# The drive factors of a selective scan: from two VectorE products to one GpSimd product per group

## The reference, cut to what matters

```python
x = _silu(conv(x_in @ W_in[:, :256]))        # u, 256 channels
delta = softplus(x @ W_dt + b_dt)
dA  = exp(delta_t[:, :, None] * A[None])     # 16 states of each channel
dBu = delta_t[:, :, None] * B_t[:, None, :] * u_t[:, :, None]
h = dA * h + dBu                             # step after step over 256 tokens
y = einsum('bds,bs->bd', h, C_t)
out = ((y + x * D) * _silu(z)) @ W_out + inp
```

## Time and profile before

| | |
|---|---|
| time before | 1379.05 us, median of 3 runs (1378.56 to 1383.14) |
| the profiled execution | 1382.59 us, span 1380.8 us |
| mean granted TensorE clock in it | 0.834 of full |
| scan phase | up to about 522 us of the span |
| a group of the scan phase | 59.8 us (from the gating at 99.82 to that at 458.65, six groups) |
| DVE busy over the span | 983.4 us (71%) |
| POOL busy over the span | 807.8 us (59%) |

### The profile page before, as it was taken

How to read it: one execution, slowest core, us unless ns; L and a number is a source line. 1 busy time by engine, 2 the same in 40 slices (tenths; PEclk the granted TensorE clock), 3 DMA queues, 4 the chain that set the end, 5 groups by cost and what they waited for, 6 DMA issues and landing times. The chain is left out here.

```text
span 1380.8 us, 15697 instructions
## 1 busy us (share of the span) xinstructions
PE 1053.1 (76%) x4347; PEld 505.1 (37%) x4347; DVE 983.4 (71%) x1673; ACT 704.0 (51%) x1392; POOL 807.8 (59%) x784
## 2 busy tenths in 40 slices
PE   6879788897988665675754778877877788649996
PEld 2334233342423223353531334333433333325554
DVE  3899999999999996656431545565666665338997
ACT  3657475675857533233331344454445453448773
POOL 1999898989989963353424333444444431237773
PEclk9899899999989896677865677787888787769998
DMA  5553241533325104000001221121122111000001
GB/s 194 220 192 155 91 185 63 214 129 148 155 91 196 51 0 90 1 0 0 0 0 46 80 60 47 58 77 52 46 60 78 47 47 47 2 0 1 16 16 31
DMA packets 34545, 103.05 MB, mean 75 GB/s; under 512 B 3611, under 2 KB 22171, under 8 KB 23707
## 3 DMA queue, kind: packets, MB, share of 16 engines
q1 hardware_dynamic: 34484, 102.35, 21.4%
HBM read 93.03 MB, written 8.91 MB: 74 GB/s over the span
## 5 line engine op out<-in xcount | busy, mean ns | idle before, releaser
L545 PE MATMUL m_yac<-m_hC,ident 128*128 128x512 f32 x512 | 283.9, 674 | 76.6 <-DVE m_hC L311 58.7
L510 POOL TENSOR_TENSOR m_dBu<-m_du,m_Bt 128x512 f32<-128x512 f32 x256 | 318.2, 1271 | 9.5 <-DVE m_du L316 8.8
L1275 ACT ACTIVATE a_pT<-a_s 128x512 f32<-128x512 f32 x256 | 150.6, 598 | 221.9 <-PE a_s L1326 221.7
L1098 DVE TENSOR_REDUCE a_nm<-a_s 128x2 f32<-128x512 f32 x256 | 163.1, 683 | 139.7 <-PE a_s L1326 136.2
L302 DVE TENSOR_TENSOR_SCAN m_dA<-m_dA,m_dBu 128x512 f32<-128x512 f32 x184 | 220.0, 1215 | 15.9 <-ACT m_dA L448 14.7
L545 PEld LDWEIGHTS m_yac<-m_hC,ident 128*128 128x128 f32 x512 | 95.2, 207 | 244.7 <-DVE m_hC L311 134.6
L448 ACT ACTIVATE m_dA<-m_delta,mprm 128x510 f32<-128x510 f32 x256 | 169.0, 673 | 0.2
L1326 PE MATMUL a_s<-qs,ks 99*128 99x256 bf16 x512 | 108.7, 307 | 44.4 <-DMA qs<-a_nmT 37.6
L1326 PE MATMUL a_s<-ks,qs 72*128 72x256 bf16 x512 | 113.5, 331 | 29.5 <-DVE a_nm L1098 18.5
L311 DVE TENSOR_TENSOR m_hC<-m_dA,m_Ct 128x512 f32<-128x512 f32 x184 | 122.6, 666 | 0.0
L445 ACT ACTIVATE m_dA<-m_zero 128x2 f32<-128x2 f32 x181 | 31.1, 172 | 166.9 <-DVE m_hC L311 166.9
(11 more groups left out here) (211 smaller groups left out, 1897.1 us busy)
## 6 DMA issues: line engine op xcount, KB each, us to landing
m_Bt<-bcd SPq DMA_DIRECT2D x32, 1024.0 KB, 5.6
m_Ct<-bcd SPq DMA_DIRECT2D x32, 1024.0 KB, 6.6
qs<-parts SPq DMA_DIRECT2D x16, 576.0 KB
ks<-parts SPq DMA_DIRECT2D x48, 192.0 KB
parts<-a_part SPq DMA_DIRECT2D x32, 192.0 KB, 2.3
out<-x_all SPq DMA_DIRECT2D x8, 256.0 KB, 2.3
mprm<-in_mprm SPq DMA_DIRECT2D x1, 1203.0 KB, 6.5
vx<-in_vrow SPq DMA_DIRECT2D x3, 256.0 KB
```

Source lines behind the costliest of these rows:

```text
L510: nc.gpsimd.tensor_tensor(dBu[:, g % RD], du[:, n % 2, c], Bt[:, s], ALU.mult).then_inc(drive_ready, 1)
L545: return nc.tensor.matmul(out, lhsT, rhs, start=start, stop=stop)
L1098: nc.vector.tensor_reduce(nm[:, q, 2 * pair:2 * pair + 2], s1[i % 2][:], AX.X, ALU.max, negate=True).then_inc(max_ready, 1)
L1275: nc.scalar.activation(pT[:, u // 2, u % 2], s2[u % 2][:], ACT.Exp, scale=float(HD) ** -0.25).then_inc(exp_ready, 1)
```

## The change

The sum of delta becomes one instruction on POOL for both halves of the channels. The drive factor moves from DVE to POOL, one instruction for both halves as well, two units behind the sum (at i = 28; in the first group directly behind the sum). The semaphores are raised by 2 at once, so that their counts are the same.

```diff
 # DVE queue
-            def drive_factor(m, c):
-                dve.wait_ge(delta_ready, CH * m + c + 1)
-                nc.vector.tensor_tensor(du[:, m % 2, c], delta[:, m % 2, c], u[:, m % 2, c],
-                                        ALU.mult).then_inc(du_ready, 1)
...
-            for c in range(CH):
-                drive_factor(0, c)
...
-                    if i in (27, 28) and n + 1 < GROUPS:
-                        drive_factor(n + 1, i - 27)
 # POOL queue
-            def sum_delta(m, c):
+            def sum_delta(m):
                 pool.wait_ge(sp_step, 7 * m + 7)
-                nc.gpsimd.tensor_tensor(delta[:, m % 2, c], sp_a[:, c], sp_r[:, c], ALU.add).then_inc(delta_ready, 1)
+                nc.gpsimd.tensor_tensor(delta[:, m % 2], sp_a[:], sp_r[:], ALU.add).then_inc(delta_ready, CH)
+
+            def drive_factor(m):
+                pool.wait_ge(delta_ready, CH * (m + 1))
+                nc.gpsimd.tensor_tensor(du[:, m % 2], delta[:, m % 2], u[:, m % 2], ALU.mult).then_inc(du_ready, CH)
...
-            for c in range(CH):
-                sum_delta(0, c)
+            sum_delta(0)
+            drive_factor(0)
...
-                    if i in (26, 27) and n + 1 < GROUPS:
-                        sum_delta(n + 1, i - 26)
+                    if i == 26 and n + 1 < GROUPS:
+                        sum_delta(n + 1)
+                    if i == 28 and n + 1 < GROUPS:
+                        drive_factor(n + 1)
```

## The result

The kernel after takes 1383.53 us (median of 12 runs) where the kernel before takes 1379.04 us in runs beside it: ratio 1.0032, 95% interval 1.0019 to 1.0044. The change costs 4.5 us; 6.3 us were forecast. The span of the profiled execution is 1381.8 us.

The account below looks back on a forecast made before the run. The group period was taken as bound by POOL's gapless queue from product 13, then factors, drives, shift, scan 31, PE's accumulation and gating. 6 x 0.88 + 1.0 = 6.3 us on 1379.05 gave 1385.4 us; range 1371.5 to 1390.

Parts of the forecast that it names:

- The price of the wide instructions: On POOL, one 1024-element instruction was taken at 2.32 us, from a line between 512 and 1120 elements.
- POOL's queue sets the period: At the six group changes behind groups 1 to 6, POOL's longer queue makes each period 0.88 us longer, 5.3 us together.
- The shift takes the place of the factors: Before scan 31, DVE's shift is held until POOL idles after drive 3, lasting some 4.7 us in place of 0.44.
- Rival (a): At the group changes, shift enters at the next end of a POOL instruction; faster, 1372 us, chance 0.23.
- Group 0: First group, without a shift: POOL is the bound and the gating behind it comes later, taken as +1.0 us.
- PE's clock: PE's accumulation before the gating: waits of about 1.04 us in three of six groups may move, -3.1 to +3.1, taken as 0.
- rival (b): Before the gating, PE waits vanish in all groups while six changes cost 0.88 us each; no change, 1382.3 us, chance 0.12.
- The sum: Whole kernel: 6 x 0.88 + 1.0 = 6.3 us slower, forecast 1385.4 us, chance 0.58.
- it runs in POOL's first idle moment: A DVE instruction with two SBUF inputs doesn't run while POOL passes between instructions without idling; shift would last some 4.7 us.

## Why the prediction was right, and where it was not

- *The price of the wide instructions* (2.36 us, from a line between two sizes): measured 2.35 and 2.36. Their gain over two narrow ones, 0.11 to 0.14 us, is in line with the run with the wide sum alone.
- *POOL's queue sets the period, up by 0.88 us:* from product 13 to product 31 it was 0.85 us. With half a factor more, 1.15 of 1.19 us appeared in this stretch.
- *The shift takes the place of the factors as the instruction that is held, 4.7 us:* 4.79 to 4.82 us. This was the step on which the sign hung, and the pause and the one-tensor form showed it by taking it away: 14 and 16 us less than the kernel after. Rival (a) had 1372 us for exactly this case; both forms came out 3 to 5 us below.
- *Group 0, +1.0 us:* the gating starts at 100.48 in place of 99.82, +0.7, inside the 100.0 to 101.0 of the forecast.
- *PE's clock, taken as 0, bounds of 3.1 us to either side:* behind groups 1 to 6 it was -0.6 us. This also decides against rival (b), whose 1382.3 us is nearer to the measured 1383.5 us than the forecast's 1385.4: it needs all of these waits gone, and 2.57 of 3.14 us are still there. The same term came out at +2.1 us in the run with the halves (5.25 against 3.14 us). Where in the group PE's clock changes level is the one part of this kernel's time that I can't work out from a diff.
- *The sum:* the last gating of the six groups starts 463.69 - 458.65 = 5.0 us later in the trace, and the runs differ by 4.5 us, with an interval of 2.6 to 6.1 us; 6.3 lies just above it. The terms as measured, 6 x 0.85 + 0.7 - 0.6 = 5.2 us, give the trace; that the runs show somewhat less is not explained by them.

The way it was reasoned was right in what it needed and wrong in its wording: "it runs in POOL's first idle moment". Four of the runs show the shift entering between two back-to-back instructions of POOL: those with the pause for the factors, the shift behind scan 31, the earlier pause, and half a factor more. And the number of tensor inputs does not draw the line: the statistics' instruction, with one, was held for 6.73 us once. The Trainium skill, "SBUF — State Buffer", section "Who interferes with whom", says that issue order decides who blocks. The traces agree in so far as POOL's instruction had started first wherever a DVE instruction was held. If POOL has instructions issued ahead of the one that runs, an exclusive port served in order of issue would pass over DVE as long as those last, and a stop would clear them; that would agree with the runs with a recent stop. It is a guess: no run here shows what POOL has issued ahead, and two places don't fit easily, the sixth change of the run with half a factor more and the statistics that were held in one group and not in the next at the same distances. What decides whether a boundary opens behind a long run of POOL stays open.

## What to carry to other kernels

Before work is moved from DVE to POOL, look for small DVE instructions that read two SBUF tensors: a POOL queue that has lost its last pause can hold one of four elements for several microseconds, and the profile books that as busy time of DVE. Compare the duration of such an instruction with that of its like elsewhere, and set its end beside the ends of POOL's instructions. If it is on the path, give POOL a wait on it just where it comes, put all such instructions at one pause, or try a form with per-partition scalars, as the four instructions of 128x1 here. One tensor input alone is no safeguard, as the 6.73 us of the statistics show.

## What was not expected of the hardware

- Four `tensor_scalar` instructions of 128x1 with a scalar from SBUF ran at 0.20 us each in the middle of a POOL instruction with two SBUF inputs, while a `scalar_tensor_tensor` of 128x4 on the same data took 4.8 us.
- A wait added to the queue that sets the period made the kernel faster by 14 us (1383.53 to 1369.31).
- A DVE instruction held by POOL ended at boundaries of a busy POOL within 0.9 us when POOL had stopped 0.4 or 4.4 us earlier. With the last long stop 29 to 31 us before, the shift was held until the next stop in 22 of 23 cases without an added pause.
- The same instruction at the same distances from POOL's stops and boundaries, to within 0.05 us, was held for several microseconds in one group and entered at the next boundary in another; this is seen in two of the runs.
